# One PSUM bank in place of two for the side jobs of two attentions

## The reference

```python
# layer 0
h = layernorm(x) * (1 + ca) + sa
q, k, v = heads(h), heads(h @ Wk + bk), heads(h @ Wv + bv)   # 16 heads, q and k 8 wide, v 32 wide
o = softmax(q k^T + causal) v
x = x + ga * (h + gelu(o) @ Wf + bf)
h = layernorm(x) * (1 + cb) + sb
x = x + gb * (shared(h) + top-2 of 8 experts(h))
# layer 1
h = layernorm(x) * (1 + ca) + sa
q, k, v = rotary(h @ qkv)      # 16 heads of 8
heads 0-5:   softmax(q k^T / sqrt(8)) v
heads 6-9:   softmax(1 / (eps + arccosh distance(q, k))) v    # hyperbolic
heads 10-15: softmax(cosine(q, k) * sqrt(8)) v
x = x + ga * (y @ proj + b)
h = layernorm(x) * (1 + cb) + sb
x = x + gb * (shared(h) + top-4 of 16 experts(h), by groups)
```

## Time and profile before

| | |
|---|---|
| median of 3 runs | 2613.69 us (2610.66 to 2616.26) |
| profiled execution | 2615.24 us |
| its span in the profile | 2613.4 us |
| TensorE busy | 2153.7 us (82%) |
| DVE busy | 1480.0 us (57%) |
| ACT busy | 1344.2 us (51%) |
| POOL busy | 833.0 us (32%) |
| mean granted TensorE clock | 0.838 of full speed |

### The profile page before, as it was taken

One profiled execution on the slowest core, in us unless ns is written; L12 is line 12 of the kernel. 1 busy time (PEld: TensorE's weight loads), 2 busy tenths in 40 slices (PEclk: granted clock), 3 DMA queues, 4 the chain that ended last, 5 costly groups with the idle time before them and its releaser, 6 DMA issues. The chain is left out here.

```text
span 2613.4 us, 29921 instructions
## 1 busy us (share of the span) xinstructions
PE 2153.7 (82%) x10649; PEld 856.6 (33%) x10649; DVE 1480.0 (57%) x3042; ACT 1344.2 (51%) x1923; POOL 833.0 (32%) x909
## 2 busy tenths in 40 slices
PE   2799877778999896677999987767899998677889
PEld 1233432224433242223443333222344324322243
DVE  2564356776555255775656525667655634577552
ACT  1155437884235534797324453579523454378922
POOL 1012213562422212553331121355233111145534
PEclk9599867678999986777899988667799998676789
DMA  4300221102400023100431012210051002301012
GB/s 133 71 19 2 67 79 34 35 1 63 135 28 20 1 82 97 35 1 1 128 92 25 2 34 77 69 36 1 13 156 50 20 2 82 82 16 35 1 50 89
DMA packets 67845, 128.31 MB, mean 49 GB/s; under 512 B 11396, under 2 KB 24836, under 8 KB 63076
## 3 DMA queue, kind: packets, MB, share of 16 engines
q1 hardware_dynamic: 67696, 126.40, 17.4%
HBM read 109.99 MB, written 15.20 MB: 48 GB/s over the span
## 5 line engine op out<-in xcount | busy, mean ns | idle before, releaser
L1333 DVE TENSOR_REDUCE mx<-ps 128x1 f32<-128x512 f32 (+3 forms) x992 | 612.4, 655 | 375.9 <-PE ps L675 244.4
L1081 ACT ACTIVATE pr<-ps 128x1024 f32<-128x1024 f32 (+3 forms) x672 | 515.2, 804 | 389.6 <-PE ps L745 388.9
L672 PE MATMUL ps<-kop,qop 72*128 72x512 bf16 (+6 forms) x1248 | 428.6, 377 | 100.1 <-DVE mx L1333 69.2
L745 PE MATMUL ps<-qop,kop 75*128 75x512 bf16 (+7 forms) x1344 | 409.4, 368 | 113.3 <-DVE wb L1395 41.1
L1622 POOL TENSOR_SCALAR_AFFINE_SELECT pr<-pr 128x512 f32<-128x512 f32 x224 | 144.4, 645 | 765.9 <-ACT pr L1081 765.1
L791 PE MATMUL ps<-pr,vt 128*32 128x512 f32 (+3 forms) x2688 | 341.3, 585 | 6.8 <-POOL pr L1622 6.4
L1142 ACT ACTIVATE pr<-ps 128x512 f32<-128x512 f32 x224 | 133.8, 597 | 342.0 <-PE ps L898 278.4
L672 PEld LDWEIGHTS ps<-kop,qop 72*128 72x128 bf16 (+1 forms) x1248 | 129.4, 106 | 434.2 <-DVE mx L1333 255.4
L745 PEld LDWEIGHTS ps<-qop,kop 75*128 75x128 bf16 (+1 forms) x1344 | 122.0, 105 | 353.6 <-ACT pr L1081 117.6
L908 PE MATMUL ps<-pr,w_down 128*128 128x512 f32 x384 | 196.5, 598 | 4.1 <-POOL pr L1613 4.1
L895 PE MATMUL ps<-hT,w_gate 128*128 128x512 f32 x384 | 196.2, 592 | 0.2 <-DVE on L1560 0.2
(11 more groups left out here) (313 smaller groups left out, 3088.9 us busy)
## 6 DMA issues: line engine op xcount, KB each, us to landing
wb<-gates_scratch SPq DMA_DIRECT2D x192, 256.0 KB, 3.3
kop<-kparts_scratch SPq DMA_DIRECT2D x32, 576.0 KB
qop<-qparts_scratch SPq DMA_DIRECT2D x96, 192.0 KB
on<-hmax_scratch SPq DMA_DIRECT2D x8, 1024.0 KB, 5.7
kparts_scratch<-on SPq DMA_DIRECT2D x12, 256.0 KB, 2.9
qparts_scratch<-on SPq DMA_DIRECT2D x12, 256.0 KB, 4.4
qparts_scratch<-wb SPq DMA_DIRECT2D x12, 192.0 KB
kparts_scratch<-wb SPq DMA_DIRECT2D x12, 192.0 KB
```

The source lines that it names most:

```text
L672: mm = pe.matmul(o, qop[0:k, slot(l, u), j, qb * P:(qb + 1) * P], kop[0:k, slot(l, u), j, k0:k0 + wd], start=True, stop=not diag)
L745: mm = pe.matmul(o, kop[0:k, slot(l, u), 2 * pair + j, kb * P:(kb + 1) * P], qop[0:k, slot(l, u), 2 * pair + j, q0:q0 + wd], start=True, s ...
L1081: nc.scalar.activation(pr[:, g % 3, 2 * pair:2 * pair + 2, o0:o0 + wd], ps[:, bank:bank + 2, o0:o0 + wd], ACT.Exp).then_inc(a.exps, 1)
L1333: ins_ = nc.vector.tensor_reduce(mx[:, nth(l, u) % 2, j0:j0 + heads, qb, col % 2], ps[:, bank, 0:heads * wd].rearrange("p (j n) -> p j n", ...
```

## The change

All side jobs write bank 7. Because there is only one bank, a job now waits for the result of the job right before it, from the second job on.

```diff
-def side_bank(g):
-    return (6, 7)[g % 2]
+def side_bank():
+    return 7
```

```diff
                         if l == 0 and more:
                             pe.wait_ge(fs[1].gates, NC)
-                    elif g >= 2:
-                        pe.wait_ge(a.side_out, g - 1)
-                    bank = side_bank(g)
+                    else:
+                        pe.wait_ge(a.side_out, g)
+                    bank = side_bank()
                     if kind == "piece":
```

## The result

| | before | one bank |
|---|---|---|
| median | 2612.18 us (4 runs) | 3275.35 us (4 runs, 3271.75 to 3282.31) |
| ratio, 95% interval | | 1.2567 (1.2534 to 1.2601) |
| span of the profiled execution | 2613.4 us | 3269.6 us |
| mean granted TensorE clock | 0.838 | 0.738 |

The forecast was 3190 us (2950 to 3345), a loss of 576 us; the loss is 663. The instructions are the same 29921. These are the stretches of the changed kernel that answer to the earlier trace rows, with the same columns. The fourth is the next unit; the sixth is the whole second attention of batch 0, which took 209.20 us before.

The account below looks back on a forecast made before the run. TensorE was taken to bound the first attention and feed-forward, DVE the stretch before the first scores, no engine full in the second attention. 205 + 3 + 132 + 51 + 6 + 26 + 153 = 576 us on 2615.2: 3190 us (2950 to 3345).

Parts of the forecast that it names:

- The round trip: First attention, units 1 to 3: jobs start 1.18 us apart instead of 0.59, 29 short gaps, 17.1 us a unit.
- "out" jobs: Two copies of the former output in three batches, beside the first attention: 3 us.
- The clock in these units: First attention, units 1 to 3: clock falls to mean 0.72, +11 us a unit, 132 in all, between 0 and 192.
- the clock stays: Rival: the clock stays where it is, giving 3052 us; chance 0.18.
- Unit 0: First attention's unit 0: 51 us wait plus 6 clock inside feed-forward, batches 1 to 3; 26 us alone in batch 0.
- The second attention: Second layer's attention: waits cost 38 us per batch, 153 in all, bounds 60 and 250.
- (a): Second attention, 11 pieces before the scores at the low clock: 7.0 us, of which 5.3 not hidden.
- (b): Second attention, 47 pieces beside the first hyperbolic halves in ten positions: 20 us, bounds 8 and 28.
- (c): Second attention, 38 pieces in nine positions: third job 1.1 us late in each, 12 us with tails, bounds 4 and 29.
- The second attention absorbs its part: Rival: ACT bounds the second attention, so its waits there cost nothing, 3062 us; chance 0.10.
- No change: Rival: TensorE slack at the jobs covers the waits, 2614 us; chance 0.02.
- Faster: Rival: DVE without a reduce backlog starts its hyperbolic chain sooner, gaining up to 66 us, 2548 us; chance 0.02.

Follow-up runs that it names:

- the filled run: One bank everywhere, up to three small unread matmuls added before reduce waits in first attentions' units 1 to 3, against unfilled one bank; 3114.08 us.
- two banks filled: Kernel before, two banks everywhere, with two small unread matmuls and an earlier bank wait ahead of each second-attention score job; 2622.71 us, ratio 1.0066.
- one bank filled: One bank in the second attention alone, with small unread matmuls added ahead of its reduce waits, against the same without them; 2690.94 us, ratio 1.0340.

## Why the prediction was right, and where a term was off

*The round trip.* 0.43 + 0.69 + 0.06 = 1.18 us predicted; 1.17 measured between job starts at full clock. The step from a mean gap of 0.59 to 1.18, 29 times a unit, gave 17.1 us; the filled run shows 18, and the unit above has 29 waits. With the "out" jobs the wait's part of the first attentions was predicted as 208 us, and it is 208.

*The clock in these units.* Predicted +11 us a unit at a mean of 0.72; in the unit shown the clock is 0.72 and the part 11 (62.2 - 51.2). That it is this very number is luck. The 0.72 was carried over from rows of the second attention, and the twelve units ran at 0.60 to 0.75, those of batch 0 in the run with two banks and the longer wait at 0.79 to 0.81. The sum over the four attentions was 132 and is 160: 150 of it in the units, of which the first of each attention is the slowest (up to 70.5 us from first reduce to last), and 10 in the other positions, which the sum left out. The rival "the clock stays" (3052 us) is refuted by the drop of 161 us on filling, not by the clock row alone.

*Unit 0.* In the feed-forward part 51 + 6 predicted, 53 measured; the 6 us of clock were unneeded, the clock is 1.00 (834.90 to 912.50 above). In batch 0 26 predicted, 26 measured. Alone in a kernel the two cost 71.

*The second attention is the step that was mis-sized.* Predicted 38 us a batch, all of it wait, no clock; measured 55 (221 / 4). By the filled runs the wait is about 17 (12 to 22) and the clock about 38. The wait was taken too large and the clock at nothing, and the two errors partly made up for each other; that the total stayed near is luck here. I had written the clock term for the units at 1.00 and let the stage at 0.74 stand as if it could fall no further; it fell to 0.60. By its parts, in batch 0, from the first reduce of a group of pieces to the end of the last (us):

| pieces | before | one bank | two banks filled | one bank filled |
|---|---|---|---|---|
| (a) 11 ahead of the scores | 7.8 | 14.9 | 7.8 | 14.9 |
| (b) 47 in positions 0 to 9 | 67.0 | 94.1 | 69.9 | 78.3 |
| (c) 38 in positions 13 to 21 | 72.0 | 90.1 | 63.5 | 73.3 |

Term (a), 7.0, is right. Terms (b) and (c) were put at 20 and 12: they are 27 and 18 as the kernel runs, and 8 and 10 with the clock held on both sides. The lower bound of 60 for the whole term is also below what its parts add up to (18.3 a batch, 73).

Position by position the wait was also read incompletely. This is the changed kernel's position that answers to the earlier trace rows, TensorE, then DVE:

```profile
678.85 0.61 PE L672 MATMUL ps<-kop,qop 72*128 72x512 bf16 x1 [1.62 <-DVE mx L1333]
...
680.25 0.61 PE L672 MATMUL ps<-kop,qop 72*128 72x512 bf16 x1 [0.36 <-DVE mx L1333]
680.78 1.94 PE L791 MATMUL ps<-pr,vt 128*32 128x512 f32 x8
...
685.95 0.28 PE L672 MATMUL ps<-kop,qop 72*128 72x256 bf16 x1 [0.79 <-DVE mx L1333]
...
675.55 1.22 DVE L1395 TENSOR_SCALAR wb<-ps 128x1024 f32<-128x1024 f32 x1
676.81 1.38 DVE L1400 SCALAR_TENSOR_TENSOR hT<-wb 128x1024 f32<-128x1024 f32 x1
678.12 0.68 DVE L1333 TENSOR_REDUCE mx<-ps 128x1 f32<-128x512 f32 x1
...
687.11 1.21 DVE L1395 TENSOR_SCALAR wb<-ps 128x1024 f32<-128x1024 f32 x1
```

The second job starts 0.73 us after the start of the reduce it waits for, and the third 1.40 after the second, as the step said but at 1.2 GHz. The first reduce stands behind two long DVE operations (675.55 and 676.81), and TensorE waits 1.62 us for it. The tail has a second job as well (685.95, waiting 0.79). It starts 1.61 us after the first (684.34); in the kernel before the two started at 527.42 and 528.03, 0.61 apart. That is 1.0 us a position, where the step allowed 2 us for the tails of all nine. DVE's operation of line 1395 comes 11.56 us after the one before (675.55 to 687.11); in the kernel before these two stood at 520.19 and 529.68, 9.49 us. So it is 2.1 us a position and not 1.1, the clock's part included. With the clock held on both sides the whole stage loses 16 us in batch 0 (230.2 against 214.4).

*The rivals.* "The second attention absorbs its part" (3062 us): not so, it lost 221 us. "No change": the loss is 663 us. The Trainium skill's report that stood beside it ("TensorE: Matmul & The Clock Gate", "HAM oscillation — how this bites in real kernels": double-buffering PSUM gave no further gain) does not carry over: here the second bank is worth a factor of 1.257. "Faster" through a shorter backlog on DVE: no run isolates it; if it exists it is smaller than what the waits cost. That the change is the wait and not the bank was my reading of the code, and the run with two banks and the longer wait shows it.

## What to carry to other kernels

A second bank is worth the round trip minus the present distance of two jobs, for each job that stands less than a round trip behind the one before, if the engine that waits is full there. Count those jobs, not all jobs. Then ask what the new pauses do to TensorE's clock, in every stage, also in one whose clock already alternates: here that was about half of the whole loss (some 160 + 150 of 663 us). To separate the two, fill the waits with matmuls that nobody reads, on the changed kernel and on the one before: what comes back was the clock, what stays is the wait. The filling costs something itself (21 or 42 us here), so the split is a range.

## What the runs showed of the hardware

Adding work can shorten a kernel: 168 more matmul records in a unit (239 to 407) made it 11 us shorter, at a clock of 1.00 in place of 0.72. The reverse trap was not expected: with the side jobs spread, TensorE was busy 0.85 of a unit and had 9.0 us of waits for reduces, and the clock still averaged 0.67; the same order with filled pauses ran at 1.00 and took 47.4 us in place of 61.4. The busy share of a stretch is therefore not to be read without the clock beside it: here slow matmuls filled it. Nor does a wait always cost clock: the feed-forward stretch with pieces got its waits too (57.2 to 74.6 us) and stayed at 1.00.
